# The last phase of an attention and MoE kernel on one Trainium2 core: sums through PSUM, statistics for two groups at once, orders written out

## What is computed

```python
slot = flat * C + jnp.minimum(pos, C - 1)          # C = 96: overflowing tokens share slot 95
buf = jnp.zeros((E * C, H), x.dtype).at[slot].set(x[tok]).reshape(E, C, H)
...
yk = out[slot].reshape(T, K, H)
y = jnp.sum(yk * topk_w[..., None].astype(yk.dtype), axis=1)
shared = jax.nn.silu(x @ Sg.T) * (x @ Su.T) @ Sd.T
...
x = x + _layernorm(ffn(...), axis=-1)              # ffn = y + shared, layer norm without weights
```

## Time and profile before

| | us |
|---|---|
| median of 3 runs | 1427.18 (1426.16 to 1430.74) |
| the profiled execution | 1425.61 |
| its span in the trace | 1423.9 |
| PE busy | 1216.2 (85%) |
| POOL busy | 930.3 (65%) |
| DVE busy | 894.6 (63%) |
| ACT busy | 831.9 (58%) |
| the last phase: last scatter issued to the end | 1343.5 to 1423.9 |

### The profile page before, as it was taken

The page is one execution under the profiler, slowest core; times in us unless marked ns, Lnnn a source line. Parts: engine busy times, 40 slices in busy tenths (PEclk is TensorE's granted clock), DMA queues, the critical chain, the costliest instruction groups (busy, mean ns, idle before and its releaser), DMA issues.

```text
span 1423.9 us, 25616 instructions
## 1 busy us (share of the span) xinstructions
PE 1216.2 (85%) x7792; PEld 845.4 (59%) x7792; DVE 894.6 (63%) x2465; ACT 831.9 (58%) x2256; POOL 930.3 (65%) x1114
## 2 busy tenths in 40 slices
PE   2588999899899899999999999999767999998921
PEld 1355656566566666666666666666534677887711
DVE  5677657578678768767877875776745322222197
ACT  2476558677676776867777776777633322332222
POOL 3587546468787886977887788798624524444553
PEclk9899999999999999999999999999888999999855
DMA  5466697645645454454444444444335278899472
GB/s 198 111 160 160 176 223 149 149 89 113 133 101 104 83 110 94 77 105 91 79 85 80 90 86 77 76 78 91 69 94 153 78 213 227 224 260 241 92 228 86
DMA packets 364488, 182.70 MB, mean 128 GB/s; under 512 B 287248, under 2 KB 343030, under 8 KB 364352
## 3 DMA queue, kind: packets, MB, share of 16 engines
q1 hardware_dynamic: 344240, 165.66, 49.6%
q0 software_dynamic: 16416, 11.70, 4.5%
q10 hardware_dynamic: 3696, 3.67, 0.8%
HBM read 75.32 MB, written 64.69 MB: 98 GB/s over the span
## 4 chain that ended last, share of the span: by engine, by line
PE 29%; POOL 18%; issue 14%; DVE 13%; ACT 12%; DMA 12%; another core or an unknown queue 1%; SPq 0%; POOLq 0%; ACTq 0%; DVEq 0%
POOL PH L879 6%; POOL P L874 6%; PE bank L924 6%; DMA Y<-W,wix 6%; DMA PT<-PH 5%; ACT P L1154 4%; POOL BUF L617 4%; PE bank L953 4%; PE bank L968 3%; PE bank L1030 3%; PE bank L939 3%; PE bank L1087 3%; PE bank L1100 2%; PE bank L985 2%; PE bank L1046 2%
## 5 line engine op out<-in xcount | busy, mean ns | idle before, releaser
L879 POOL TENSOR_TENSOR PH<-P,PH 128x512 f16<-128x512 f32 x256 | 301.0, 1176 | 167.1 <-ACT PH L1163 164.5
L924 PE MATMUL bank<-RB,W 128*128 128x512 f16 x1092 | 278.6, 381 | 17.2 <-DVE RB L366 13.9
L953 PE MATMUL bank<-RB 128*128 128x256 f32 x1024 | 254.4, 391 | 33.9 <-DVE RB L1259 13.1
L874 POOL TENSOR_SCALAR P<-P,rr 128x256 f32<-128x256 f32 x512 | 246.5, 490 | 46.1 <-DVE rr L1280 46.1
L617 POOL DMA_INDIRECT BUF<-RT,ix x192 | 203.5, 1060 | 89.8 <-issue 35.4
L1154 ACT ACTIVATE P<-bank,nm 128x256 f32<-128x256 f32 x512 | 237.4, 473 | 25.5 <-DVE nm L1284 18.4
L968 PE MATMUL bank<-PT,RB 128*128 128x256 f16 x1536 | 212.3, 275 | 34.9 <-DVE O L1290 26.0
L953 PEld LDWEIGHTS bank<-RB 128*128 128x128 f32 x1024 | 185.8, 193 | 71.5 <-issue 23.2
L1163 ACT ACTIVATE PH<-P 128x512 f16<-128x512 f32 x256 | 163.2, 637 | 86.5 <-POOL P L874 50.3
L968 PEld LDWEIGHTS bank<-PT,RB 128*128 128x128 f16 x1536 | 146.5, 98 | 107.5 <-issue 46.0
L1146 ACT ACTIVATE O<-bank,bqk 128x256 f16<-128x256 f32 x256 | 122.9, 480 | 130.1 <-PE bank L968 126.2
(11 more groups left out here) (176 smaller groups left out, 1676.6 us busy)
## 6 DMA issues: line engine op xcount, KB each, us to landing
RB<-in_ewT SPq DMA_DIRECT2D x34, 352.0 KB
HT<-in_ewT SPq DMA_DIRECT2D x25, 352.0 KB
BUF<-zrow SPq DMA_DIRECT2D x4, 1926.0 KB, 8.8
W<-BUF SPq DMA_DIRECT2D x64, 120.4 KB
HT<-in_wc SPq DMA_DIRECT2D x24, 256.0 KB, 3.6
HT<-in_ws SPq DMA_DIRECT2D x24, 256.0 KB, 4.1
RB<-in_ewd SPq DMA_DIRECT2D x34, 176.0 KB
Y<-zrow SPq DMA_DIRECT2D x9, 512.0 KB, 3.1
```

The source lines that it names most:

```text
L874: r = eng.tensor_scalar(p, p, rr[:, w % 4, t:t + 1], SP_, ALU.mult, ALU.mult)
L879: eng.tensor_tensor(PH[:, w % 2, 1, :], P[:, w % 2, :], PH[:, w % 2, 0, :], ALU.subtract).then_inc(s["pl"], 1)
L924: r = eng.matmul(bk_[:, :], W[:, m, a, c * 2048 + h * 128:c * 2048 + (h + 1) * 128], XT[:, bp % 2, b, c, :], start=(k == 0), stop=(k == n ...
L953: r = eng.matmul(bS[u % 2][:, t * 256:(t + 1) * 256], QK[:, i % 2, 0, q * 256 + t * 128:q * 256 + (t + 1) * 128], QK[:, i % 2, 1, q * 256: ...
```

## The change

The last phase no longer uses `final_jobs` and its chains; each engine's order is written out.

- Banks: group g uses pair g % 4 of LB_ (the same eight banks, in another order).
- PE: `last_over(g)` makes the four matmuls with OUT95 and leaves the sum open; for group 7 it then adds YL by four matmuls with the 128 x 128 identity matrix as weights. `last_add(g)` waits until POOL has formed Y0 + Y1 and adds it into the same banks by four identity matmuls (128 x 128 by 128 x 256, f32). The order is over 0, 1, 2, 3, then add 0, 1, 2, 3, over 4, add 4, over 5, add 5, over 6, add 6, over 7, add 7. From group 4 on, `last_over` waits until ACT has read the banks of group g - 4.
- POOL: the sums Y0 + Y1 (s) and the first halves of + x1 (x) in the order `s0 s1 s2 s3 x0 s4 x1 s5 x2 x3 s6 s7 x4 x5 x6 x7`. YL is no longer added here.
- DVE: bn_stats reads PSUM, and L694 has no counterpart. The twelve small instructions are issued once for a batch, on 128 x 8 values for two groups: batches (0,1), (2,3), (4,5), (6), (7). Behind each batch come the second halves of + x1 of the batch before.
- ACT: normalises from PSUM to SBUF and signals after each half of a group, so that POOL's half can start after two tiles.
- SP: the stores wait for both halves of their group. The loads are as before.

```diff
-LEAD = (2, 0, 8, 10)
+BATCH = ((0, 1), (2, 3), (4, 5), (6,), (7,))
+POOL_LAST = "s0 s1 s2 s3 x0 s4 x1 s5 x2 x3 s6 s7 x4 x5 x6 x7"
...
-        def final_jobs(g):
...
+        LB_ = ((bACC[0], bACC[1]), (bV, bO), (bS[0], bS[1]), (bP0, bP1))
...
+            def last_sum(g):
+                f = fin[g]
+                eng.wait_ge(s_fl[g], 32)
+                for h in range(2):
+                    r = eng.tensor_tensor(half(f[:, 0], h), half(f[:, 0], h), half(f[:, 1], h), ALU.add)
+                r.then_inc(s["fa"], 1)
+
+            def last_x1(g):
+                f = fin[g]
+                eng.wait_ge(s["fn"], 2 * g + 1)
...
+                eng.tensor_tensor(half(f[:, 0], 0), half(f[:, 0], 0), half(x1[g], 0), ALU.add).then_inc(s["fx"], 1)
+
+            for name in POOL_LAST.split():
+                (last_sum if name[0] == "s" else last_x1)(int(name[1:]))
...
+            def last_over(g):
+                if g >= 4:
+                    eng.wait_ge(s["fn"], 2 * (g - 4) + 2)
+                for t in range(4):
+                    eng.matmul(LB_[g % 4][t // 2][:, t % 2 * 256:(t % 2 + 1) * 256],
+                               W95T[:, (4 * g + t) * 128:(4 * g + t + 1) * 128], OUT95[0:E, :],
+                               start=(t % 2 == 0), stop=False, skip_group_check=True)
+                if g >= LATE:
+                    for t in range(4):
+                        eng.matmul(LB_[g % 4][t // 2][:, t % 2 * 256:(t % 2 + 1) * 256], ident[:, :],
+                                   YL[g][:, t, :], start=False, stop=False, skip_group_check=True)
+
+            def last_add(g):
+                eng.wait_ge(s["fa"], g + 1)
+                for t in range(4):
+                    r = eng.matmul(LB_[g % 4][t // 2][:, t % 2 * 256:(t % 2 + 1) * 256], ident[:, :],
+                                   fin[g][:, 0, t, :], start=False, stop=(t % 2 == 1), skip_group_check=True)
+                r.then_inc(s["fp"], 1)
+
+            for g in range(4):
+                last_over(g)
+            for g in range(NP):
+                if g >= 4:
+                    last_over(g)
+                last_add(g)
...
+            for g in range(NP):
+                eng.wait_ge(s["fs"], batch_of(g) + 1)
+                for h in range(2):
+                    for t in (2 * h, 2 * h + 1):
+                        c = 4 * g + t
+                        r = eng.activation(fin[g][:, 0, t, :], LB_[g % 4][h][:, t % 2 * 256:(t % 2 + 1) * 256],
+                                           ACT.Identity, bias=fNW[:, 3, c:c + 1], scale=fNW[:, 1, c:c + 1])
+                    r.then_inc(s["fn"], 1)
...
+            def step(ins):
+                ins.then_inc(s["fd"], 1)
+                fd[0] += 1
+                eng.wait_ge(s["fd"], fd[0])
+
+            def last_stats(gs):
+                for g in gs:
+                    eng.wait_ge(s["fp"], g + 1)
+                    for t in range(4):
+                        r = eng.bn_stats(fST[g][:, t, :], LB_[g % 4][t // 2][:, t % 2 * 256:(t % 2 + 1) * 256])
+                step(r)
+                c0, c1 = 4 * gs[0], 4 * gs[-1] + 4
+                for c in range(c0, c1):
+                    r = eng.bn_aggr(fMV[:, c, :], fST[c // 4][:, c % 4, :])
+                step(r)
+                v, y, a, b = (fNW[:, k, c0:c1] for k in range(4))
+                step(eng.tensor_scalar(v, fMV[:, c0:c1, 1], EPS, None, ALU.add))
+                step(eng.tensor_scalar(y.bitcast(I32), v.bitcast(I32), -0.5, RSQRT_MAGIC, ALU.mult, ALU.add))
+                for k in range(3):
+                    step(eng.tensor_tensor(a, y, y, ALU.mult))
+                    step(eng.scalar_tensor_tensor(out=b, in0=a, scalar=-0.5, in1=v, op0=ALU.mult, op1=ALU.mult))
+                    step(eng.scalar_tensor_tensor(out=y, in0=b, scalar=1.5, in1=y, op0=ALU.add, op1=ALU.mult))
+                eng.scalar_tensor_tensor(out=b, in0=fMV[:, c0:c1, 0], scalar=-1.0, in1=y, op0=ALU.mult, op1=ALU.mult
+                                         ).then_inc(s["fs"], 1)
...
+            for n, gs in enumerate(BATCH):
+                last_stats(gs)
+                if n:
+                    for g in BATCH[n - 1]:
+                        last_x1(g)
+            for g in BATCH[-1]:
+                last_x1(g)
```

More of the change, by code:

```diff
@@ L199, in build @@
         Af = A[:, :, :].rearrange("p t n -> p (t n)")
[L200 to L205, removed]
+        ST = [st[:, k, :, :] for k in range(2)]
+        MV = [mv[:, k, :, :] for k in range(2)]
+        NW = [nw[:, k, :, :] for k in range(2)]
+        fST = [Af[:, g * 24:(g + 1) * 24].rearrange("p (t n) -> p t n", t=4) for g in range(NP)]
+        fMV = Af[:, 192:256].rearrange("p (t n) -> p t n", t=32)
+        fNW = Af[:, 256:384].rearrange("p (k t) -> p k t", k=4)
         gm0 = sb("gm0", [128, 4])
@@ L663, in build @@
         plan["sp"].setdefault(END + 101, []).append(last_rows)
-        fin_out = {}
-        def final_jobs(g):
[L669 to L687, removed]
-            if g >= LATE:
-                for h in range(2):
-                    yield ch.step("pool", slot, lambda e, h=h: e.tensor_tensor(
-                        half(f[:, 0], h), half(f[:, 0], h), half(YL[g], h), ALU.add))
-            yield from [0] * LEAD[0]
-            for h in range(2):
-                yield ch.step("dve", slot, lambda e, h=h: e.tensor_tensor(
-                    half(f[:, 0], h), banks[h][:, :], half(f[:, 0], h), ALU.add))
-            yield from [0] * LEAD[1]
-            yield from stats(ch, 2 + b, [slot] * 4, lambda t: f[:, 0, t, :])
-            yield from normal(ch, 2 + b, slot, lambda t: f[:, 0, t, :], lambda t: f[:, 0, t, :])
-            yield from [0] * LEAD[2]
-            w = [(s["po"], PO_END)] if g >= 4 else [(s["xr"], 64)]
-            for h, who in enumerate(("pool", "dve")):
-                fin_out[g] = ch.step(who, slot, lambda e, h=h: e.tensor_tensor(
-                    half(f[:, 0], h), half(f[:, 0], h), half(x1[g], h), ALU.add), w)
-                yield
@@ L706, in build, with half, batch_of @@
-        jobs = [final_jobs(g) for g in range(NP)]
[L707 to L710, removed]
+        LB_ = ((bACC[0], bACC[1]), (bV, bO), (bS[0], bS[1]), (bP0, bP1))
+        def half(a, h):
+            return a[:, 2 * h:2 * h + 2, :].rearrange("p t n -> p (t n)")
+        def batch_of(g):
+            return [g in b for b in BATCH].index(True)
         def run_plan(who, eng, slot, k=0, n=1):
@@ L836, in _ @@
             for g in range(NP):
-                eng.wait_ge(s_fc[g % 4], fin_out[g])
+                eng.wait_ge(s["fx"], g + 1)
+                eng.wait_ge(s["fy"], g + 1)
                 eng.dma_start(out[g * 512:(g + 1) * 512, :].rearrange("(t p) d -> p t d", p=128), fin[g][:, 0, :, :]
@@ L1112, in _ @@
                     pe_piece[INTO[e][0]](INTO[e][1])
-            run_plan("pe", eng, 1000)
+            eng.wait_ge(s["wtc"], NP)
+            for k in range(4):
+                eng.wait_ge(s_o95[k], 16 * E // 4)
+            def last_over(g):
[21 more added lines that the diff above has]
+                last_add(g)
         @block.scalar
```

18 lines of the change are left out of this document (12 added, 6 removed).

## The result

The changed kernel took 1411.89 us (median of 4 runs, 1409.78 to 1415.79) against 1428.12 us before (median of 4, 1426.16 to 1430.74). The ratio is 0.9888, 95% interval [0.9858, 0.9919]: 16.2 us faster by the medians, where 15.0 had been forecast (1412.2 from 1427.2).

The account below looks back on a forecast made before the run. DVE, with its holds beside POOL's adds, was taken to bound the last phase. The schedule put the last store 16.2 us earlier; less 1.2 for hand-overs, gain 15.0: profiled 1410.6, median 1.6 above, 1412.2 us; range 1409 to 1415.

Parts of the forecast that it names:

- DVE was the bound, and the holds: Last phase: DVE busy 9.79 of 10 us; each POOL add holds one small DVE instruction, about 1.2 us instead of 0.16.
- DVE's work after: Last phase: DVE's statistics, small instructions and x1 adds take 30.6 us in place of about 55, plus holds.
- DVE therefore no longer bounds by work: Last phase: with 30.6 us of DVE work plus holds, the chain of hand-overs is what counts.
- DVE still busy over 9 of 10 us: Sign in the profile after that the forecast was wrong, pointing to rival B or D.
- B: Last phase: dearer holds, or full PSUM cost and ACT at 2.07; gain 3 to 9 us, about 1421 us; chance 0.09.
- D: Last phase: written order makes POOL stand so long that DVE waits for it; gain 0 to 3 us; chance 0.05.
- Reading PSUM: Last phase: bn_stats from PSUM costs 0 extra (bounds 0 to 60 ns each); ACT 0.85 us for two tiles, 1.65 for four.
- The clock: PE, last phase: full clock returns during add 0 near 1359, drops around over 4 and add 6, returns after each.
- The ends: End of last phase: last store issued at 1401.8 instead of 1418.0; about twelve hand-overs give 1.2 us back.
- because PE was idle: Last phase: the add through PE, open group and explicit order cost little of themselves.
- A: PE, last phase: clock stays at 0.50 to the end; gain 10.7 us, about 1416.5 us; chance 0.20.
- C: PE becomes the bound, identity weight loads not hidden, 6.1 us a group; 24 us slower, 1451 us; chance 0.04.

Follow-up runs that it names:

- the second profile of the change: The changed kernel run and profiled once more, unchanged: ratio 0.9859 [0.9835, 0.9883] to the kernel before; last phase 60.4 us, against 59.0 in the first profile.
- order and pairs: Changed kernel without PE's identity adds of Y; DVE adds PSUM and the Y sum into SBUF: ratio 0.9903 to the kernel before, last phase 60.9 us.

## Why the prediction was right

To set the schedule beside the profile I take both from the start of POOL's first sum, 1352.56 in the forecast and 1356.23 in the profile after, that is 3.67 us later.

| | forecast | measured - 3.67 |
|---|---|---|
| ACT starts batch (0,1) | 1366.5 | 1366.35 |
| batch (2,3) | 1376.6 | 1376.27 |
| batch (4,5) | 1387.3 | 1387.6 |
| batch (6) | 1393.4 | 1394.0 |
| batch (7) | 1398.9 | 1399.35 |
| last store | 1401.8 | 1402.3 |

**DVE was the bound, and the holds.** Right. One small instruction is held for each POOL add: four and part of a fifth in batch (2,3), where five were forecast; unheld ones start 0.20 us apart. Taking POOL's sums away took all holds but one away. In batch (4,5), where four were forecast, only one was (0.80 us), because DVE came to it late, after its wait for PE.

**DVE's work after.** The sum of 30.6 us was right, with one thing I had not asked: whether a small instruction on 128 x 8 costs more than one on 128 x 4. It took 0.17 against 0.16 us. The comparison and the conclusion were not. The "about 55" of before is DVE's busy time with its holds in it (55.6 us from 1356.6 to 1413.8, of them 17.7 held), so without holds some 38 stand against 30.6. And "DVE therefore no longer bounds by work" is contradicted by the trace, and by my own schedule, in which DVE has no free place from 87.3 on: behind its wait for PE, from 1386.11 to 1403.02, the chain that ended last is all DVE. "DVE still busy over 9 of 10 us" was one of my signs of being wrong, and it came in two of the three windows (9.55 and 9.35), without B or D being true. It was a bad sign: the schedule from which the number comes had DVE full as well. So the number rests on the schedule, not on that sentence.

**Reading PSUM.** bn_stats from PSUM took 415 ns (32 of them), from SBUF 410: 5 ns, near my 0. The 65 ns of the Trainium skill (VectorE: DVE Perf Modes, "The TRN2 errata") do not show here. ACT was mis-sized: 572 ns and not 473, so four took 1.93 us (1.65 taken, 2.07 from SBUF), and the first half was signalled after 1.1 us instead of 0.85. L1154, from which I took 473, is another activation; that was the nearest row by memory but not by function. It changed the sum little, since POOL's and DVE's halves overlap more than I had them (DVE's add took 0.94 us beside POOL's and ended 0.55 behind it, where I had 0.69): from ACT's last start to the last store it was 2.97 us, forecast 2.9.

**The clock.** The first step held: the clock came back as add 1 began (1363.1, that is 1359.4 on the forecast's scale, forecast 1359) and dropped during over 4, before which PE had stood for 2.2 us (1369.7, forecast 1369). The next did not: I had it back after add 4, and it stayed at 0.50 for 13.65 us:

```profile
1359.69:1363.10 3.41, 3.41 (x9) 2.70 (x8) 0.52 (x2) 0.00 (x0) 2.88 (x3) 0.50 1.10 347
1363.10:1366.51 3.41, 3.29 (x15) 2.41 (x14) 2.67 (x12) 0.00 (x0) 2.88 (x4) 0.98 1.11 350
1373.34:1386.99 13.65, 13.17 (x30) 8.68 (x29) 9.60 (x21) 4.18 (x9) 10.53 (x10) 0.50 0.46 151
1386.99:1397.23 10.24, 9.03 (x39) 6.80 (x37) 9.42 (x42) 3.75 (x8) 4.56 (x4) 0.99 0.30 102
```

From 1359.69 PE ran 128 x 128 adds alone, and the clock rose at 1363.1; from 1373.34 overs of 64 partitions and adds of 128 took turns, PE nearly gapless, and it did not for 13.65 us. Nor is that a rule: the same turns, gapless at 0.50, reached full clock within two groups in the kernel with all sums first (from 1373.58; over 5 at 1380.68 took 2.01 us) and in the second profile of the change (1.00 from 1382.64). The second drop that I had put around add 6 did not come here (1.00 for add 6, over 7, YL and add 7), and came in the second profile. When the clock falls and rises in such a mixed stretch stays open; I did not forecast it, and that it cost so little was the holds' doing. The sum survived because of the sentence that batch (4,5) would be ready at 87.3 or, at half clock, at 87.7. That was right in amount (87.6) and for its reason: what PE loses, the holds would have taken, as OUT95 on 128 partitions showed.

**The ends.** Hand-overs were put at 1.2 us; the last store was 0.5 us behind the schedule. So close a hit is in part luck: on the same scale the second profile's last store lies 2.1 us behind the schedule, 0.9 more than the 1.2. POOL's two adds of a sum took 2.48 us and not 2.60, which fits that no step of a chain stands between them in the new code.

**Rivals.** A, half clock to the end, happened in part: in the second profile of the change the end was at half clock and cost 1.4 us of phase, far less than the 4.3 that I had priced for half clock everywhere (1416.5 - 1412.2). B did not come. C was excluded: the groups of eight took 3.7 to 3.8 us at half clock and 1.9 to 2.0 at full, the weight loads hidden. D's opposite was true, as far as one profile shows it: the written order is worth 2.9 us alone, 1.1 of them at the end, and without it the adds on PE would have made the kernel 1.7% slower. That the parts need each other so much I had not said: I had called PE's adds nearly free "because PE was idle", which is true of its time but not of its place in the ring.

## What to carry to other kernels

When work is moved to an idle engine, draw the ring of waits that it closes before counting its time: the same adds on PE cost 24 us in the old order and saved 5.5 in the new one, and once the order is right, two ways of relieving the same engine do not add up. If POOL and DVE run side by side in SBUF, count one small DVE instruction held for each POOL instruction, and join small instructions of several tiles into one, since twice the values cost 0.01 us. Two chains in turns on one engine hide part of each other's steps (0.15 us a step here, 0.19 for one chain alone), so an order written out one chain after another should join them in return. A wait behind which another hold is due is worth little when it goes: 3.7 us of PE came back as 0.6. And when a forecast adds up an engine's work after a change, set beside it the work before without its waits and holds, and see whether the schedule leaves that engine any free place before calling it relieved.

## What the runs showed of the hardware

- Gapless f32 matmuls of 64 partitions left the clock at 0.50: before, it fell at 1342.17 in the middle of them and stayed down to 1353.65, and in the change the 32 records took 13.99 us, all at 0.50, and 13.99 us again in five other forms. The same ones padded with zeros to 128 partitions had it back from 1347.79 on, 0.97 on average (8.83 us for 32 records, and 9.49 and 8.83 in the two other forms that have them). The Trainium skill (TensorE: Matmul & The Clock Gate, "The HAM clock gate") speaks of sustained activity only; here two equally gapless streams differed. Groups of 64 and of 128 partitions in turns did either: at 0.50 for 13.65 us in the change, back at full clock after two groups in three other profiles.
- Where the low stretch falls differs from one execution of a kernel to the next: 1373.3 to 1387.0 in one, 1375.8 to 1382.6 and again 1389.5 to 1403.1 in the other.
- Held DVE instructions end with POOL's add (1373.66 + 1.18 beside POOL's 1372.34 + 2.48), and bn_stats and bn_aggr beside a POOL add keep their 0.41 and 0.15 us; so do DVE's adds with an operand in PSUM (0.64 us each with order and pairs).
